# Taking out 160 idle matmuls that run in TensorE's quiet stretches (two transformer layers with a mixture of experts, one core)

## The reference

```
x = layernorm(x + L0_attn(x))   # 16 heads of 16, 4 key heads, rotary, band |i-j| <= 64, sink in the score
x = layernorm(x + L0_ffn(x))    # silu(x Wg) * (x Wu) Wd, 1024 wide, int8 weights with scales
x = layernorm(x + L1_attn(x))   # 16 heads of 16, rotary, causal, biases
x = layernorm(x + L1_ffn(x))    # 2 of 16 experts of width 176, and a shared one of width 352
```

## Time and profile before

| | us |
|---|---|
| median of the runs (lowest, highest) | 1183.8 (1180.29, 1187.39) |
| profiled execution: span from its first to its last instruction | 1160.3 |
| around the span (median less span) | 23.5 |
| TensorE busy | 850.7 (73% of the span) |
| VectorE busy | 638.3 (55%) |
| mean granted TensorE clock | 0.849 of full |

### The profile page before, as it was taken

The page is one execution under the profiler, slowest core; times in us unless marked ns, Lnnn a source line. Parts: engine busy times, 40 slices in busy tenths (PEclk is TensorE's granted clock), DMA queues, the critical chain, the costliest instruction groups (busy, mean ns, idle before and its releaser), DMA issues.

```text
span 1160.3 us, 17749 instructions
## 1 busy us (share of the span) xinstructions
PE 850.7 (73%) x5446; PEld 649.8 (56%) x5447; DVE 638.3 (55%) x1510; ACT 457.1 (39%) x960; POOL 372.4 (32%) x595
## 2 busy tenths in 40 slices
PE   2577888967787898888888879788872088898700
PEld 2465765646567556666755566575541077777500
DVE  4472487456248755634676572467635045576555
ACT  1444433753442365353346544324540033444300
POOL 5033440321443132052422324242221460122274
PEclk9598889988888997797989897898985588999955
DMA  9200000000000000000000000000008931233233
GB/s 320 103 3 1 19 1 1 2 20 4 1 20 1 1 2 1 22 2 19 1 1 2 2 20 2 1 1 1 2 19 239 234 134 36 70 129 119 91 112 105
DMA packets 38438, 54.06 MB, mean 47 GB/s; under 512 B 8504, under 2 KB 32824, under 8 KB 37488
## 3 DMA queue, kind: packets, MB, share of 16 engines
q0 software_dynamic: 8192, 27.43, 7.6%
q1 hardware_dynamic: 22464, 18.62, 5.9%
q10 hardware_dynamic: 7696, 6.91, 1.9%
HBM read 24.76 MB, written 20.71 MB: 39 GB/s over the span
## 4 chain that ended last, share of the span: by engine, by line
PE 40%; issue 25%; POOL 13%; DVE 11%; another core or an unknown queue 4%; ACT 3%; DMA 2%; ACTq 0%; POOLq 0%; DVEq 0%
POOL prob L518 5%; PE ps L1298 5%; DVE negmax L970 4%; PE ps L1534 4%; PE ps L1312 4%; PE ps L1189 3%; PE ps L1285 3%; POOL fT L528 3%; PE ps L1174 3%; PE ps L1461 2%; PE ps L1551 2%; POOL back L576 2%; PE ps L1224 2%; PE ps L1417 1%
## 5 line engine op out<-in xcount | busy, mean ns | idle before, releaser
L970 DVE TENSOR_REDUCE negmax<-ps 128x2 fp32r<-128x512 f32 (+4 forms) x304 | 178.3, 630 | 77.5 <-PE ps L1285 75.8
L707 ACT ACTIVATE prob<-ps 128x448 f32<-128x448 f32 (+2 forms) x320 | 157.9, 536 | 65.1 <-PE ps L1298 58.7
L1285 PE MATMUL ps<-kT,qT 128*128 128x256 f32 (+4 forms) x512 | 157.8, 391 | 0.0
L513 POOL TENSOR_TENSOR carry_p<-neg_half 128x1 f32<-128x1 f32 x80 | 16.4, 205 | 350.9 <-ACT prob L707 350.9
L1298 PE MATMUL ps<-qT,kT 128*128 128x192 f32 (+4 forms) x512 | 123.1, 330 | 2.5 <-ACT prob L707 1.2
L518 POOL TENSOR_SCALAR_AFFINE_SELECT prob<-prob 128x512 f32<-128x512 f32 (+1 forms) x192 | 109.6, 599 | 0.0
L615 ACT ACTIVATE xT<-ps 128x256 fp32r<-128x256 f32 x100 | 37.6, 387 | 173.7 <-PE ps L1182 173.0
L1298 PEld LDWEIGHTS ps<-qT,kT 128*128 128x128 f32 x512 | 84.6, 202 | 37.1 <-ACT prob L707 24.8
L1285 PEld LDWEIGHTS ps<-kT,qT 128*128 128x128 f32 x512 | 102.2, 214 | 3.4
L1312 PE MATMUL ps<-prob,v_aug 128*32 128x256 f32 (+4 forms) x1024 | 79.9, 421 | 12.4 <-POOL prob L518 12.0
L821 DVE TENSOR_TENSOR xT<-ps,xT 128x256 fp32r<-128x256 f32 x100 | 41.1, 422 | 69.2 <-ACT xT L615 68.9
(11 more groups left out here) (180 smaller groups left out, 1821.4 us busy)
## 6 DMA issues: line engine op xcount, KB each, us to landing
slot_x<-zeros ACTq DMA_DIRECT2D x1, 6016.0 KB, 31.5
xs_sb<-slot_x SPq DMA_DIRECT2D x47, 128.0 KB, 2.0
slot_y<-ys_sb POOLq DMA_DIRECT2D x47, 128.0 KB, 2.0
w_sb<-in_w POOLq DMA_DIRECT2D x4, 1408.0 KB, 25.6
w_sb<-in_w POOLq DMA_DIRECT2D x5, 704.0 KB, 24.4
x<-in_x SPq DMA_DIRECT2D x4, 512.0 KB, 3.7
qT<-shift_row SPq DMA_DIRECT2D x128, 2.0 KB, 1.7
x_rows<-x SPq DMA_DIRECT2D x4, 512.0 KB, 3.2
```

The costliest lines, as they stand in the source:

```text
L707: act.activation(prob[:, part % PROB_BUFS, j, 0:n], ps[:, 3 + i % 3, 0:n], ACT.Exp, scale=SCALE).then_inc(exped[l].sem, 1)
L970: dve.tensor_reduce(out=negmax[:, t, s * GH + j * mh:s * GH + (j + 1) * mh], in_=ps[:, k % 3, 0:mh * n].rearrange("p (h n) -> p h n", n=n) ...
L1285: ins = pe.matmul(dst[:, jj, :], qT[:, h // 2, t * P:(t + 1) * P], kT[:, k_block(h), k0:k0 + n], start=False, stop=True, skip_group_check= ...
```

## The change

The three counts are set to zero. Nothing else is touched; the loops over zero matmuls issue nothing.

```diff
-IDLE_HEAD, IDLE_TAIL, IDLE_FFN = 10, 4, 4
+IDLE_HEAD, IDLE_TAIL, IDLE_FFN = 0, 0, 0
```

## The result

The changed kernel takes 1198.3 us (median, 1196.4 to 1202.46, 4 runs). The kernel before, run beside it, takes 1182.05 us (1179.62 to 1187.39). The ratio is 1.0125, with a 95% interval of 1.0081 to 1.0168. It is an estimate over the runs and not the quotient of the two medians: by it the kernel is slower by 14.8 us, by the medians by 16, where 14.1 were forecast. A second measurement gave 1.0141 (1.0102 to 1.018).

A forecast was written before the change was run, and what follows sets the result against it. TensorE was taken to be on the path (40% of the chain), partly at 1.2 GHz. Stacking and step 0 +7.4, feed-forward start +3.8, between batches +2.9 made +14.1 us: 1197.9 us, range 1184 to 1211.

The forecast's parts named there:

- The fillers' own time, and the clock, in the stacking: Layer 1's stacking: 6.3 us of filler time comes back, while tiles 2 and 3 at 1.2 GHz cost 11.1 us.
- The 11.1 of the sum: Layer 1's stacking: cost in all batches of tiles 2 and 3 at the low clock, 2.7 us a batch or slightly more.
- Rival one: Layer 1's stacking: clock returns by itself, fillers only cost time; 1175 to 1177 us, decided at tile 2's q; chance 0.12.
- the second rival: Gains and losses cancel: clock low for tile 2 only, feed-forward part begins as before; about 1185 us; chance 0.18.
- Step 0 of layer 1: Raw scores begin at the low clock: 4.5 us of it, costing 0.65 us a batch, 2.6 in all.
- grows by under 1 us: Sign for the profile after: step 0 of layer 1 lengthens by less than 1 us.
- the bound of 1.0 a batch: Step 0 of layer 1: upper bound on its low-clock cost, in us, for two low stretches.
- The third rival: Low clock lasts into layer 1's step 2, +6.4 us: 1204, or 1207 with all feed-forward starts low longer; chance 0.17.
- Feed-forward start: Gate matmuls: clock rises one low stretch later; +3.8 us in all, bounds -0.4 and +6.5.
- The term for batch 3: Feed-forward start of batch 3: if the clock drops it costs 1.7 us, counted at half.
- Between batches: Ahead of batch 3, clock drops over last stacking and layer 0's step 0: +2.9 us; other edges 0.
- with the 23.5 us around the span: Whole kernel: 23.5 us added to the forecast span of 1174.4 us to give 1197.9.

The follow-up runs named there:

- e1: Changed kernel with idle matmuls put back only in layer 1's stacking (10, 0, 0); ratio to the kernel before 1.0051 (1.0019 to 1.0082).
- e3: Changed kernel with idle matmuls put back only at the batch edges (0, 4, 0); ratio to the kernel before 1.0126 (1.0089 to 1.0163).
- e6: Kernel before, layer 1's stacking refilled (9, 16, 8, then 6 idle matmuls), plus 7, 1, 5, 0 ahead of x1's transposed tiles; 1174.95 us, ratio 0.9928.
- e7: Kernel before, its idle matmuls untouched, plus 7, 1, 5 and 0 ahead of the four transposed tiles of x1; ratio 0.9951 (0.9921 to 0.9982).
- e5: Kernel before with 9, 16, 8 idle matmuls ahead of tiles 1, 2, 3 and 6 behind in layer 1's stacking, instead of 0, 10, 10, 10; ratio 0.9986.

## Why the prediction was right, point by point

That the total is met to 0.4 us (1197.9 against 1198.3) is luck in part. The median of before fell by 1.75 us between the forecast and the result, as one more run came in. And the places that the forecast counted cost more than it said, 20.7 us in the traces against 14.1, while places that it had at nothing gave 8.2 back. The mechanism is shown, place by place; the agreement of the sum is not its proof. Sums over four batches, from both profiles of each kernel (mean before, mean after), beside the terms:

| | before | after | change | forecast |
|---|---|---|---|---|
| layer 1's stacking | 79.0 | 83.9 | +4.9 | +4.8 |
| step 0 of layer 1 | 28.0 | 32.2 | +4.2 | +2.6 |
| gate and up matmuls | 63.1 | 68.9 | +5.8 | +3.8 |
| from there to the next stacking | 94.0 | 91.8 | -2.2 | 0 |
| batch edges and step 0 of layer 0 | 97.6 | 103.4 | +5.8 | +2.9 |
| steps 1 and 2 of layer 1 | 64.8 | 67.3 | +2.4 | 0 |
| layer 0, step 1 to the first gate matmul | 242.5 | 234.7 | -7.8 | 0 |
| the rest of layer 1 | 134.3 | 133.7 | -0.6 | 0 |

Each row is a sum of the stretches between the first or last instruction of its lines; they add up to the 12.5 us of part 1, against 14.8 by the ratio; two profiles each, whose part 1 differs by up to 6 us within one kernel, do not tell these apart. The first profile of each kernel starts its raw scores at 55.73 and 58.32 us, the second at 56.25 and 55.61, so the start is no part of it.

*The fillers' own time, and the clock, in the stacking.* Right in mechanism and size: +1.7 us in batch 0, where 2.7 - 1.1 = 1.6 had been worked out. (The 11.1 of the sum is 0.4 more than four times 2.67, and no row was named for it.) Tile 3's pair took 3.65 us (181.27 to 184.92), tile 2's 3.99; forecast 3.67. Rival one, the clock coming back by itself, was decided at tile 2's q, as said: from 175.43 to 184.92 it is 0.50. That puts the second rival out as well, which needed it to be up for tile 3.

*Step 0 of layer 1.* The term was too small by both its factors. A mean clock of 0.65 over 8.14 us is 0.70 x 8.14 = 5.7 us at the low clock, where 4.5 were counted, and 8.14 - 6.99 = 1.15 us for these is 0.20 per microsecond, where step 1 had shown 0.14. The sign "grows by under 1 us", and the bound of 1.0 a batch, failed in this batch and in one more. VectorE idled 8.14 - 6.61 = 1.5 us instead of 6.99 - 6.13 = 0.9, so TensorE bounds some of this step at 1.2 GHz. That it does so more here than in step 1, whose first items VectorE finds ready, is argued and was not tested. It is 1.05 us a batch against 0.65.

*Steps 1 and 2.* The third rival, the low clock lasting into step 2, came true now and then: that step took 10.3 us in batches 0 and 2 of the first profile after and in one batch of the second, the others 8.7; before, in batch 0 of the first profile alone. With what step 1 lost it is +2.4 us, not the rival's +6.4.

*Feed-forward start.* Right in kind. The low clock lasted 0.30 x 17.25 = 5 us into the gate matmuls in batch 0. The term for batch 3 was 1.7 us, counted at half; it came in at 2.7 (14.93 to 17.63 us), and batches 0 and 1 lost 1.3 and 1.6. Part came back: before, batches 0 and 1 met a low stretch in layer 1's projections that the changed kernel does not have there (24.00 against 22.57 us); in the second profile before, it was batches 2 and 3. A drop moved is not a drop added.

*Between batches.* The edge from batch 2 to 3: stacking 0.86 later and step 0 of layer 0 7.38 against 5.37, together +2.9, the forecast to 0.1 in the first profile. In the second it is 24.11 against 19.88 and 6.66 against 5.38, together +5.5, with the clock low from the edge's start. The other two edges, forecast 0, ran low or high as it fell: 23.07 and 26.30 us before, 26.22 and 22.56 after. Where they ran high they took 23.0 to 23.1 before and 22.6 after, so at most 0.5 us a jump came back.

*What was not foreseen* is the -7.8 in layer 0. Before, four of eight batches took 49.2 to 49.5 us from step 3 to the first gate matmul, the others 44 to 46; after, all eight took 44 to 47. Three of the four stand in the second profile, whose execution was one of the longest of its runs; the first profiles alone give -1.8. In batch 3 of both profiles of the kernel before, the router's 24 matmuls took 5.23 us, against 3.67 in batch 0 of the first, in a long stretch at the low clock. Here it is in the first profile:

```profile
706.80:716.80 10.00, 9.96 (x55) 8.64 (x56) 0.00 (x0) 2.45 (x6) 0.19 (x1) 0.50 0.01 1
```

TensorE is busy throughout and the clock does not return. Whether a batch meets this depends on the moment, and e1, e3, e6 and e7 met it in one batch each; I cannot say that the fillers cause it.

*The sum.* One step failed without harm: "with the 23.5 us around the span". A span has 1.7 us around it (1200.8 and 1202.46). The 23.5 came from setting one short execution (a span of 1160.3, so about 1162 in all) against runs of 1180 to 1187. By the other profiles it was short in parts 2 and 3 above all (304 us, where chips of such times had 319 to 329); why it was, stays open. As the same constant stood on both sides, it cancelled.

*The page on modelling.* The Trainium skill's "<1% of a typical kernel span" (TensorE: Matmul & The Clock Gate, Part 1) stands there for the warm-up at a kernel's start. The prediction stretched it over all low stretches, and its estimate by that was a time under 1195.4; the result is 1198.3. That counts against the stretching and not against the sentence, which no run here tests. Part 4 of the same page of the Trainium skill speaks of transpose mode alone. That ordinary matmuls against a unit matrix would count was the prediction's own step. In the 9.5 us between 175.43 and 184.92 they, with the waits between them, did not lift the clock.

## What to carry to other kernels

An idle matmul in a wait can pay when what stands behind it is a chain of short TensorE work: here 160 of them cost some 6 us where they overran, and saved over 20 (an estimate: the 15 to 16 us that the kernel loses without them, and those 6). Judge a filler by the next real instruction's ready time and by the clock column of the stretch behind it, and look at the waits ahead of dense TensorE work, where filling gave another 0.5% here (e7), and 0.7% with the stacking filled otherwise (e6). Before summing on one profile, compare its span with the runs' times; where they differ by more than a few microseconds, some part of that execution was unusual.

## What the runs showed of the hardware that was not expected

- 160 matmuls of 16 columns did nothing for the clock (0.57 in batch 0's stacking, as without any), and those of 512 columns at the same places did (0.82). The short ones also fill less of the waits; which of the two it is was not tested.
- Filled waits do not by themselves keep the clock: in e5 it held over tiles 1 and 2 and dropped at 174, with fillers on both sides.
- The same program took 1162 us on one chip and 1183 to 1185 on two others. The traces put that in parts 2 and 3 (296 to 306 against 319 to 329 us), where the expert weights and the token rows are loaded. The kernel before was never profiled in an execution of over 1171 us, so for it this is argued from the other kernels.
